# Sixteen-head context attentions: keys and values from split parts, and exps over pairs of PSUM banks

## The reference, cut to what matters

```
q = x @ Wq (+ bq)        # 16 heads of 16 numbers
k = ctx @ Wk (+ bk)
v = ctx @ Wv (+ bv)
attn = softmax(q . k * 0.25) over the 1601 keys
out = (attn @ v) @ Wo (+ bo)
```

## Time and profile before

| | |
|---|---|
| median of 3 executions | 5561.72 us (5552.97 to 5569.8) |
| profiled execution, its own time | 5562.66 us |
| its span | 5560.9 us |
| granted TensorE clock, mean | 0.912 |
| TensorE busy | 4837.1 us, 87% |
| VectorE, ScalarE, GpSimd busy | 3035.0, 2118.8, 935.9 us |

### The profile page before, as it was taken

One profiled execution on the slowest core, in us unless ns is written; L12 is line 12 of the kernel. 1 busy time (PEld: TensorE's weight loads), 2 busy tenths in 40 slices (PEclk: granted clock), 3 DMA queues, 4 the chain that ended last, 5 costly groups with the idle time before them and its releaser, 6 DMA issues. The chain is left out here.

```text
span 5560.9 us, 113654 instructions
## 1 busy us (share of the span) xinstructions
PE 4837.1 (87%) x45694; PEld 3720.1 (67%) x45694; DVE 3035.0 (55%) x5687; ACT 2118.8 (38%) x4053; POOL 935.9 (17%) x473
## 2 busy tenths in 40 slices
PE   6879999998759989999766899987689989998877
PEld 4659888896549966666423788876269956665465
DVE  5358777772554455555287433354633366664443
ACT  1235555552134434444243333343034434443121
POOL 0022222220002200000076122142612200000200
PEclk8889999999669999999988899988879999999885
DMA  1010000000101111110022111022911010000110
GB/s 60 29 36 15 15 22 15 16 7 27 50 31 45 45 43 50 38 50 26 22 76 69 46 45 50 18 81 57 121 46 53 23 38 26 27 21 33 42 59 30
DMA packets 195844, 222.91 MB, mean 40 GB/s; under 512 B 43251, under 2 KB 164932, under 8 KB 187236
## 3 DMA queue, kind: packets, MB, share of 16 engines
q1 hardware_dynamic: 195428, 216.93, 13.9%
HBM read 170.09 MB, written 15.34 MB: 33 GB/s over the span
## 5 line engine op out<-in xcount | busy, mean ns | idle before, releaser
L2367 DVE TENSOR_REDUCE block_max<-PS 128x1 f32<-128x512 f32 (+1 forms) x896 | 505.5, 627 | 300.3 <-PE PS L2227 299.7
L2316 ACT ACTIVATE probs_turned<-PS 128x512 f32<-128x512 f32 (+1 forms) x896 | 434.6, 571 | 563.3 <-PE PS L2248 563.2
L1632 PE MATMUL PS<-input_part,part_up 128*128 128x512 f32 x2304 | 552.5, 393 | 18.4 <-DVEq L1713 8.6
L1645 PEld LDWEIGHTS PS<-part_down,hidden_part 128*128 128x128 f32 x4608 | 548.7, 189 | 2.0
L1645 PE MATMUL PS<-part_down,hidden_part 128*128 128x256 f32 x4608 | 549.1, 281 | 0.0
L1685 ACT ACTIVATE hidden<-PS,b 128x512 f32<-128x512 f32 x384 | 264.4, 689 | 651.7 <-PE PS L1632 637.2
L1632 PEld LDWEIGHTS PS<-input_part,part_up 128*128 128x128 f32 x2304 | 434.9, 190 | 110.1 <-DVEq L1713 9.3
L844 PE MATMUL PS<-context_turned,queries 128*128 128x512 f32 x1728 | 413.4, 384 | 25.3 <-issue 18.4
L876 PE MATMUL PS<-probs_turned,context_part 128*128 128x256 f32 (+2 forms) x3120 | 410.1, 286 | 3.7 <-DVE weighted L953 3.7
L905 ACT CAST probs_turned<-PS 128x512 fp32r<-128x512 f32 x576 | 261.2, 510 | 358.3 <-PE PS L856 358.3
L1721 DVE TENSOR_TENSOR hidden_part<-hidden,hidden_part 128x512 fp32r<-128x512 f32 x384 | 293.8, 774 | 183.1 <-ACT hidden_part L1675 182.4
(11 more groups left out here) (441 smaller groups left out, 8052.8 us busy)
## 6 DMA issues: line engine op xcount, KB each, us to landing
context_rows<-in_ctx SPq DMA_DIRECT2D x40, 768.0 KB
raw_up<-in_L_ffn_W SPq DMA_DIRECT2D x16, 1024.0 KB, 4.8
raw_down<-in_L_ffn_W SPq DMA_DIRECT2D x16, 1024.0 KB, 4.8
v_all<-v_turned SPq DMA_DIRECT2D x128, 128.0 KB, 19.4
ctx_turned<-context_turned SPq DMA_DIRECT2D x16, 800.5 KB, 4.7
context_turned<-ctx_turned SPq DMA_DIRECT2D x16, 800.5 KB
b_all<-bc_turned SPq DMA_DIRECT2D x32, 256.0 KB, 3.5
c_all<-bc_turned SPq DMA_DIRECT2D x32, 256.0 KB, 4.3
```

The lines of the kernel that those rows point to most:

```text
L1632: last = nc.tensor.matmul(PS[:, k % ring + 2 * x, :], bank.parts[name][a][:, c, f * P:(f + 1) * P], h[b][:, c, half * 512:(half + 1) * 512 ...
L1645: last = nc.tensor.matmul(PS[:, 4 + t % outs, 0:DIM], aT[a][:, f, t * P:(t + 1) * P], bank.parts["down"][b][:, f, :], start=(f == 0 and m ...
L2316: nc.scalar.activation(probs[0:kk, t % ring, i, 0:many].rearrange("p k c s -> p (k c s)"), PS[0:kk, bank_of("turned", t, i), 0:many * 2 * ...
L2367: nc.vector.tensor_reduce(part[:, b % 2, chunks[0]:chunks[-1] + 1, i, u // 2], bank, AX_X, ALU.max).then_inc(max_done.sem, 1)
```

## The change

Four things are changed in `head_attention`.

1. Context and weights are split: each number is rounded to the fp32r format (the lead part), and the remainder is kept beside it. Keys and values are then three fp32r matmuls each (`PRODUCTS`: lead by lead, lead by remainder, remainder by lead) in place of one fp32 matmul. GpSimd splits the context in four pieces a batch, by a cast and a subtraction each; ScalarE and VectorE split the two weights once a stage. Odd column counts (65) are made even (66).
2. `v_lead` goes from 10 to 3 turns and `c_lead` from 13 to 14. The values are kept in a ring of six turns in place of two whole batches.
3. Exps of two neighbouring banks of the ring are one operation. Where T0 falls on bank 4 or 6, two of the four stay single.
4. In the second stage the next context load waits for the split instead of for the last keys and values of that batch.

```diff
     total = BATCH * turns
-    s_lead, v_lead, k_lead, c_lead = 8, 10, 12, 13
+    s_lead, v_lead, k_lead, c_lead = 8, 3, 12, 14
-    ring, banks, out_bank = 3, 7, 7
+    ring, v_ring, banks, out_bank = 3, 6, 7, 7
+    pieces, even = 4, KEYS + KEYS % 2
...
-        V = core.sb(own, "values", [P, 2, KT, heads, wide])
+        V = core.sb(own, "values", [P, v_ring, 2, heads, wide])
+        yp = [core.sb(own, "context_part", [P, 2, even], F32R) for _ in range(2)]
+        wkp = core.sb(own, "wk_parts", [P, 2, DIM], F32R)
+        wvp = core.sb(own, "wv_parts", [P, 2, DIM], F32R)
...
                     elif b + 2 < BATCH:
-                        last = max(fill_no["values", b * turns + turns - 1], fill_no["keys", b * turns + turns - 1])
-                        sp.wait_ge(side_ready.sem, side_ready.at(last + 1))
+                        sp.wait_ge(y_split.sem, y_split.at((b + 1) * pieces))
...
+                for p in yp:
+                    nc.gpsimd.memset(p[:, :, KEYS:even].bitcast(F32), 0.0).then_inc(filled.sem, 1)
+                for b in range(BATCH):
+                    for j in range(pieces):
+                        n, cols = b * pieces + j, slice(512 * j, min(512 * j + 512, KEYS))
+                        if first:
+                            pool.wait_ge(side_act.sem, side_act.at(act_no["context", b * turns + j] + 1))
+                        else:
+                            pool.wait_ge(room.landed[b % 2].sem, room.landed[b % 2].at(room.per_batch * (b // 2 + 1)))
+                        if b >= 2:
+                            u = (b - 2) * turns + min(2 * j + 1, turns - 1)
+                            pool.wait_ge(side_ready.sem, side_ready.at(max(fill_no["values", u], fill_no["keys", u]) + 1))
+                        nc.gpsimd.tensor_copy(yp[0][:, b % 2, cols], room.y[b % 2][:, cols]).then_inc(y_lead.sem, 1)
+                        pool.wait_ge(y_lead.sem, y_lead.at(n + 1))
+                        nc.gpsimd.tensor_tensor(yp[1][:, b % 2, cols], room.y[b % 2][:, cols], yp[0][:, b % 2, cols],
+                                                ALU.subtract).then_inc(y_split.sem, 1)
...
                 def wait_context(b, to):
-                    if first:
-                        pe.wait_ge(side_act.sem, side_act.at(act_no["context", b * turns + to // 512] + 1))
-                    else:
-                        pe.wait_ge(room.landed[b % 2].sem, room.landed[b % 2].at(room.per_batch * (b // 2 + 1)))
+                    pe.wait_ge(y_split.sem, y_split.at(b * pieces + to // 512 + 1))
...
+                    wide_cols = cols + cols % 2
                     for n, c in enumerate(chunks):
-                        last = nc.tensor.matmul(PS[:, bank_of("keys", t), n * cols:(n + 1) * cols], wk[:, c * P:(c + 1) * P],
-                                                room.y[b % 2][:, lo:lo + cols], start=True, stop=True)
+                        for m, (x, z) in enumerate(PRODUCTS):
+                            last = nc.tensor.matmul(PS[:, bank_of("keys", t), n * wide_cols:(n + 1) * wide_cols],
+                                                    wkp[:, x, c * P:(c + 1) * P], yp[z][:, b % 2, lo:lo + wide_cols],
+                                                    start=(m == 0), stop=(m == 2))
                     last.then_inc(side_ready.sem, 1)
...
                     for n, kt in enumerate(tiles_of(j)):
-                        kk = keys_of[kt]
-                        last = nc.tensor.matmul(PS[0:kk, bank_of("values", t), n * DIM:(n + 1) * DIM], room.y[b % 2][:, kt * P:kt * P + kk], wv[:],
-                                                start=True, stop=True)
+                        kk = keys_of[kt] + keys_of[kt] % 2
+                        for m, (x, z) in enumerate(PRODUCTS):
+                            last = nc.tensor.matmul(PS[0:kk, bank_of("values", t), n * DIM:(n + 1) * DIM],
+                                                    yp[x][:, b % 2, kt * P:kt * P + kk], wvp[:, z, :],
+                                                    start=(m == 0), stop=(m == 2))
                     last.then_inc(side_ready.sem, 1)
...
-                                                        V[0:kk, b % 2, kt, 8 * a + 4 * c + i, :],
+                                                        V[0:kk, t % v_ring, n, 8 * a + 4 * c + i, :],
...
-                    for i in range(groups):
-                        nc.scalar.activation(probs[0:kk, t % ring, i, 0:many].rearrange("p k c s -> p (k c s)"),
-                                             PS[0:kk, bank_of("turned", t, i), 0:many * 2 * P], ACT.Exp,
-                                             scale=scale).then_inc(exp_done.sem, 1)
+                    i = 0
+                    while i < groups:
+                        at = bank_of("turned", t, i)
+                        both = 2 if i + 1 < groups and at + 1 < banks else 1
+                        nc.scalar.activation(probs[0:kk, t % ring, i:i + both, 0:many].rearrange("p i k c s -> p i (k c s)"),
+                                             PS[0:kk, at:at + both, 0:many * 2 * P], ACT.Exp,
+                                             scale=scale).then_inc(exp_done.sem, both)
+                        i += both
...
+                    if b >= 2:
+                        act.wait_ge(y_split.sem, y_split.at((b - 2) * pieces + j + 1))
...
+                for parts, whole in ((wkp, wk), (wvp, wv)):
+                    nc.scalar.copy(parts[:, 0, :], whole[:]).then_inc(w_lead.sem, 1)
                 nc.scalar.activation(warm[:], core.ident[0:1, 0:1], ACT.Exp)
...
-                    out = V[0:kk, b % 2, 2 * j:2 * j + many, :, 0:d]
+                    out = V[0:kk, t % v_ring, 0:many, :, 0:d]
...
+                for n, (parts, whole) in enumerate(((wkp, wk), (wvp, wv))):
+                    dve.wait_ge(w_lead.sem, w_lead.at(n + 1))
+                    nc.vector.tensor_tensor(parts[:, 1, :], whole[:], parts[:, 0, :], ALU.subtract).then_inc(filled.sem, 1)
```

More of the change, by code:

```diff
@@ L2070, in head_attention @@
     landed, stored = core.semaphore("weights_landed"), core.semaphores("context_stored", 2)
+    y_lead, y_split, w_lead = core.semaphore("context_lead"), core.semaphore("context_split"), core.semaphore("weights_lead")
     cycles = range(-c_lead, total + 6)
@@ L2285, in sums_spread @@
                                      stop=True).then_inc(side_ready.sem, 1)
-                pe.wait_ge(filled.sem, filled.at(4))
+                pe.wait_ge(filled.sem, filled.at(8))
                 for t in cycles:
@@ L2323, in keys_out @@
                     act.wait_ge(side_ready.sem, side_ready.at(fill_no["keys", t] + 1))
+                    wide_cols = cols + cols % 2
                     for n, c in enumerate(chunks):
-                        last = nc.scalar.activation(kT[:, b % 2, c, lo:lo + cols], PS[:, bank_of("keys", t), n * cols:(n + 1) * cols], ACT.Identity)
+                        last = nc.scalar.activation(kT[:, b % 2, c, lo:lo + cols],
+                                                    PS[:, bank_of("keys", t), n * wide_cols:n * wide_cols + cols], ACT.Identity)
                     last.then_inc(side_act.sem, 1)
@@ L2427, in head_attention @@
     m_ready.passed(2 * BATCH)
-    filled.passed(4)
+    y_lead.passed(BATCH * pieces)
+    y_split.passed(BATCH * pieces)
+    w_lead.passed(2)
+    filled.passed(8)
     cleared.passed(1)
```

## The result

The changed kernel takes 5573.16 us in the median (5560.31 to 5590.3, 18 runs), the kernel before 5560.68 (5540.41 to 5574.01, 18 runs). The ratio is 1.0025, 95% interval 1.0015 to 1.0034: slower by 8 to 19 us (0.0015 and 0.0034 of 5560.68). The forecast was 5563 and no change within 0.3%; the change is 0.25%, and the time lies inside the range of 5536 to 5590. It is on the slower side, clear of the noise, and those 12 us or so are to be found.

What follows compares the result with a forecast made beforehand. The prediction took the ring from T over ScalarE's exps to S as the bound. Second stage +9.5, first stage -10.5, stage ends +1 and weights' split +0.9 made +1 us: 5563 us, range 5536 to 5590.

Steps and rivals of the forecast that it cites:

- The bound: Nearly every cycle is held by the ring from T over ScalarE's exps to S; TensorE only looks full.
- Exps of two banks: On ScalarE, an exp of 1024 columns takes 1.045 us, and two pairs end after 1.975 us.
- both bounds: Two paired exps on ScalarE: at least 1.71 us by columns alone, at most 2.12 by the row of 1024 columns.
- The row of 1.119: Another attention's 1024-column exp, 1.119 us with per-row bias and sum, taken as the upper case for a pair.
- The cycles: T to next T: two pairs 5.73 us; a pair and two singles 5.28 with ten fills, 5.77 with eleven.
- from the end of an exp to the S that it lets go is 0.14: Step in every gated cycle: S starts 0.14 to 0.15 us after the exp that releases it ends.
- The short turn: Turn of 4.87 us where exps have 256 columns: cheaper V and K take the whole 0.60 us off.
- two signs: S waits for ScalarE 1.0 us with pairs, 0.55 with singles; TensorE's busy time in 490 us falls to about 410.
- Ends of a stage: Per stage, -4 us ahead of T0 and +4.5 at the end; both stages together +1.
- Splits on GpSimd: A piece takes about 1.9 us with hand-overs, against 6.9 us of cover in the first stage before K needs it.
- The sum: Whole kernel: +9.5 - 10.5 + 1 + 0.9 = +1 us, giving 5563 us.
- single rival: Faster exps 5523 (0.14), TensorE bound 5453 (0.04), slower pairs 5588 (0.12), slower clock 5624 (0.06), late splits or slower products 5583 (0.04).

Runs made afterwards that it cites:

- single_exps: Changed kernel with each exp on one bank again, split parts and leads kept: 5563.97 us, 5564.05 before, ratio 1.0002.
- one_wait: Changed kernel with S and T waiting once per semaphore, for the latest bank needed, instead of once per bank: 5572.09 us, 5564.05 before, ratio 1.0013.
- first_pair: Changed kernel with one wait per semaphore in S and T, and only T0 and T1 paired: 5549.81 us, 5564.05 before, ratio 0.9971.

## Why the prediction was right or wrong

- **The bound**: right. S is held by the exps. Taking exps in pairs in the kernel before alone cost 32 us (some 6 of them excess), and with single exps TensorE's cheaper products gave nothing in full cycles (single_exps: 5.29 to 5.34, as before).
- **Exps of two banks**: right. They took 1.023 us (I took 1.045), two of them 1.94 (1.975), inside both bounds; the estimate from the Trainium skill (ScalarE: Activation LUTs, What ACT_TABLE_LOAD costs) of 1.04 and 1.99 was as near for one exp and 0.05 high for two. The row of 1.119 was the wrong one to go by. Both stages, 2000 to 5140 us:

```profile
L2341 ACT ACTIVATE probs_turned<-PS 128x1024 f32<-128x1024 f32 x330 | 323.0, 1023 | 467.4 <-PE PS L2270 467.4
L2341 ACT ACTIVATE probs_turned<-PS 128x512 f32<-128x512 f32 x108 | 61.6, 599 | 77.4 <-PE PS L2270 77.4
```

- **The cycles**: ten fills and two pairs, 5.73 foretold, 5.71 to 5.73 measured; eleven fills with singles 5.77, measured 5.76 to 5.79. But eleven fills with two pairs took 5.83, not 5.73, and the sixth cycle of a batch stayed at 5.37, where -0.09 was foretold. The step that failed is "from the end of an exp to the S that it lets go is 0.14": one release now frees two banks, and TensorE's wait for the second is still to be done. Shown by one_wait, but for the sixth cycle in the second stage only. By the shares of the banks it is 5/7 x 4 x 0.1 in a batch of the first stage, 0.1 in the sixth cycle of both, and 5/7 x 0.1 more in the second for T0 on bank 6. For the 14 batches of T0 to T98 that is 4.0 + 2.8 + 1.0, about 8 us.
- **The short turn**: right in kind, wrong in size. The second step that failed is "I take the whole 0.60 off": the turn went from 4.87 to 4.56, 0.31. The turn runs without a wait in both kernels. From the start of V to that of K, from there to the transpose of the maxima and on to S, first before, then changed:

```profile
4801.89 1.13 PE L2212 MATMUL PS<-L_xattn_Wv,context_turned 128*128 128x256 f32 x4
4802.86 1.02 PE L2202 MATMUL PS<-context_turned,wk 128*128 128x512 f32 x2
4803.72 0.27 PE L2278 MATMUL PS<-ident,row_max 128*128 128x128 f32 x1
4803.92 1.14 PE L2227 MATMUL PS<-keys_turned,queries 32*128 32x512 f32 x8
```

```profile
4701.03 0.97 PE L2233 MATMUL PS<-wv_parts,context_part 128*128 128x256 f32 x6
4701.83 0.86 PE L2221 MATMUL PS<-context_part,wk_parts 128*128 128x512 f32 x3
4702.53 0.27 PE L2300 MATMUL PS<-ident,row_max 128*128 128x128 f32 x1
4702.73 1.14 PE L2249 MATMUL PS<-keys_turned,queries 32*128 32x512 f32 x8
```

  V went from 0.97 to 0.80 and K from 0.86 to 0.70. So of the 0.29 that is missing, V's products are 0.12 (0.80 for 0.68), K's 0.06 (0.70 for 0.64), and 0.10 is the start: K took 0.96 only where S followed it, and 0.86 here. The split V needs a new weight for each product, and six such loads span 0.77 us, 0.13 each, more than the 0.113 per product in the experts:

```profile
4825.87 0.77 PEld L2233 LDWEIGHTS PS<-wv_parts,context_part 128*128 128x128 f32 x6
```

  0.29 us in 28 short turns are 8 us. The same sizes are part of why two signs missed: S waits 0.72 us after two pairs and 0.28 after a pair and singles, where I had 1.0 and 0.55, and TensorE is busy for 441.7 us of the first window, where I had about 410.
- **Ends of a stage**: -4 and +4.5 a stage foretold, together +1 (and 0.9 for the first start). Measured from the first fill to T0 -4.4 and -4.7, from T98 to the last T +3.8 and +3.5, together -2: 4 us better.
- **Splits on GpSimd**: hidden, as foretold. 1.8 to 2.0 us a piece, and no wait of TensorE for them after the start of a stage.
- **The sum**: 1 + 8 + 8 - 4 = +13 on the numbers above. The stages have +18, of which 5 are excess, so 13 too, and the medians say 8 to 19. No single rival came true; two small terms lay on the same side. I gave "no change" for a sum of parts of +-10 us that cancel, and each part's error stayed when the parts had gone. That the errors of the terms left the total within 0.3% owes something to luck: without the 4 us at the ends it would have stood at the edge.

## What to carry to other kernels

When banks go round in a ring, find the operation whose end lets the next producer go. Fewer, wider operations help the engine that runs them, but they let go of the first bank later: merge those ahead of the one that is waited for, and not that one with its successor. When cheaper work gives nothing, look for what ends its wait. And when one release serves several waits in a row, wait once, for the last.

## What the runs showed of the hardware

- A further wait on TensorE that is pending at the release costs about 0.1 us (S 0.25 after the exps' end with two, 0.15 with one).
- A DMA burst of 8 us at 77% of the engines is followed by pauses of 0.5 to 2.5 us in TensorE's stream that no semaphore ends. The instruction transfers of 16 KB, 5.9 us apart in the median, then start 9 to 11 us apart, and each of the 48 pauses ends 1.2 to 1.6 us after one of them has landed. With store and load in four pieces, the excess of the first stage fell from 15.1 to 1.2 us (first_pair), from 15.0 to 0.8 (changed) and from 9.9 to 0.4 (before).
- Six split products of 256 columns with a new weight each took 0.80 to 0.81 us to the next piece, two fp32 products of the same size 0.97. In the short turn three of 512 columns took 0.70, one in fp32 0.86.
